# Dilation kernel: seven row sides on TensorE and ScalarE, half merges into pair tiles, 24 GpSimd pairs

## The chip, the cores and the metric

The kernel runs on one core of a Trainium2 chip. Its time is the device time of one execution in microseconds; the time before is 10253.23 us, the median of 3 runs (10250.52 to 10257.87).

## What is computed

The input x has shape 8 x 32 x 256 x 256, fp32. The reference does two residual steps:

```
x = x + dilation(gn(x))      # grey dilation, 11 x 11 taps
x = x + conv(gn(x))          # 1x1 projection, 3x3 depthwise, batch norm, gelu, offsets, bilinear resampling

dilation: acc = max over 121 taps (di, dj) of  pad(u)[y + di, x + dj] - k[channel, di, dj]
```

gn is a group norm with 16 groups of two channels. Since it is a scale and a shift per image and group, the kernel dilates the raw x with k times the standard deviation and scales the result at the end.

## The kernel before

The 256 planes (8 images x 32 channels) lie on 128 partitions in two groups. The kernel has four stages: statistics and tables (to about 200 us), the dilation (to about 8685 us), the convolution and the resampling. The change is in the dilation.

**Tiling.** A window u holds 16 rows of output with 5 rows and columns of border on each side; two windows alternate. A window is done in two chunks of 8 rows x 256 columns, so a chunk's tile is 128 x 2048 fp32. There are 64 chunks. For each window GpSimd also makes dx = u shifted by one column minus u (`difference`, L192).

**Pairs.** Two neighbouring taps of a row can be merged as max(u0 - k0, u1 - k1) = u0 + relu(u1 - u0 + k0 - k1) - k0. ScalarE makes the relu from dx (`pair_relu`, L621), the addition of u is done either by a DMA that accumulates in SBUF (16 "y" pairs in four t tiles, `add_u`, L501) or by GpSimd (`pair`, L530) in four m tiles. For the pairs in CLAMPED GpSimd makes the first part itself by a min and a max (`clamp`, L518), and then adds (L526). VectorE merges the tile into acc_a in PSUM with one instruction, (tile - k) max acc_a (`merge`, L718; the first merge of a chunk, L715, has no max). Single taps ("s") are merged straight from u.

**Chains.** One side of a row, 5 or 6 taps, can also be done as a chain in PSUM: ScalarE does the relu (`chain_step`, L639), TensorE adds the next dx or u by an identity matmul (`add_step`, L589), and so on. A chain is done in two halves of 4 rows (chain0, chain1). Before, there are six: one left with 4 steps, five right with 5 steps, 29 steps for each half. At a chain's end VectorE merges the half into a second accumulator acc_b in SBUF (`merge_chain`, L692, 128 x 1024). acc_b is started by ScalarE from one single tap (`start_b`, L606), and at the end of the chunk a join takes the maximum of both accumulators (L725), after which x1 is made (L731). SyncE stores x1 and loads the next windows.

**What sets the order.** Each engine works in order. Four strings list what each does in one chunk: ACT_ORDER (x relu for a DMA pair, r relu for a GpSimd pair, 0 and 1 chain steps of the halves, b start of acc_b, u the square sum of x1), PE_ORDER, DVE_ORDER (m, y, s merges, 0 and 1 chain merges) and POOL_ORDER (i issue of an accumulating DMA, c clamp, t addition, d pieces of dx for the next window). Semaphores bind them: an addition waits for its relu or clamp, a merge for its tile, a relu or clamp for the merge that frees its buffer (`a_free`), a chain's first step for VectorE's merge of the chain before on that half.

Of the kernel before, what the change touches and what calls it, by code (L numbers as in the profile page):

```python
# [70 lines left out]
def dilation_taps():  # L75

    pairs, singles = [], []
    for di in range(KS):
        side = dict(CHAINS).get(di)
        if side == "left":  # L80
            pairs += [(di, 5, 6), (di, 7, 8), (di, 9, 10)]
        elif side == "right":
            pairs += [(di, 1, 0), (di, 3, 2)]
            singles += [(di, 4)]
# [3 lines left out]
    while len(pairs) > NPOOL + len(CLAMPED) + NDMA:  # L88
# [269 lines left out]
def dilation(nc, x_pl, x1_pl, ident, kt, nkt, gap_r, gap_l, rstd, shift1, sums1,  # L358
# [3 lines left out]
    D_TURNS = POOL_ORDER.count("d")  # L362
    pool_pairs, dma_pairs, (init_b, *singles) = dilation_taps()
    NPAIR = NPOOL + len(CLAMPED)

# [8 lines left out]
    def col(di, dj):  # L374
        return di * KS + dj


    chain_steps = []
    for ch, (di, side) in enumerate(CHAINS):
        bases = range(1, 5) if side == "left" else range(9, 4, -1)  # L380
        chain_steps += [(ch, step, base) for step, base in enumerate(bases)]
# [8 lines left out]
    with ExitStack() as ctx:  # L390
# [8 lines left out]
        t = [sb(f"t{s}", [P, CR, UC]) for s in range(TP)]  # L399
        acc_b = sb("acc_b", [P, CR, W])  # L400
        x1 = sb("x1", [P, CR, W])
# [16 lines left out]
        chain_taken = [sem(f"chain_taken{h}") for h in range(2)]  # L418
        b_started = sem("b_started")
        a_done = sem("a_done")  # L420
        merged = sem("merged")
        joined = sem("joined")
        act_turns, sp_turns, dve_turns, pool_turns = (sem(f"{e}_turns") for e in ("act", "sp", "dve", "pool"))

        def m_tile(j):

            di, base, outer = pool_pairs[j]
            first = (di * UC + base + 2) % 4
            return m_tiles[j % MP][:, :, first:first + W]

        def at(c, per_chunk, count):
# [20 lines left out]
        with nc.Block() as block:  # L452
# [114 lines left out]
            def _(pe):  # L567
# [8 lines left out]
                def add_step(c, s, k, h, i):  # L576
                    ch, step, base = chain_steps[i]
                    di, side = CHAINS[ch]
# [12 lines left out]
                    added.then_inc(chain_added[h], 1)  # L591
# [9 lines left out]
            def _(act):  # L601
                def start_b(c, s, k):
                    di, dj = init_b

                    act.wait_ge(merged, at(c, 1, 0))
                    nc.scalar.activation(acc_b[:], u[s][:, k * CR + di:k * CR + di + CR, dj:dj + W], ACT.Identity,  # L606
                                         bias=nkt[:, g, col(di, dj):col(di, dj) + 1]).then_inc(b_started, 1)

                def square_before(c, shift_column):
# [15 lines left out]
                def chain_step(c, s, k, h, i):  # L625
                    ch, step, base = chain_steps[i]
                    di, side = CHAINS[ch]
                    right = side == "right"
# [15 lines left out]
                for g in range(GROUPS):  # L644
                    with nc.Fori(0, WIN // 2, engines=ACT_ONLY, hint_back_edge=True) as i:
                        for s in range(2):
                            n = i * 2 + (g * WIN + s)
                            for k in range(CPW):
# [4 lines left out]
                                for kind, j in numbered(ACT_ORDER):  # L653
                                    if kind in "01":
                                        chain_step(c, s, k, int(kind), j)
                                    elif kind == "r":

                                        act.wait_ge(a_done, a_free(c, "m", relu_pairs[j], NPAIR, MP))
                                        pair_relu(s, k, pool_pairs[relu_pairs[j]], m_tile(relu_pairs[j])) \
                                            .then_inc(m_begun, 1)  # L660
                                    elif kind == "x":

                                        act.wait_ge(a_done, a_free(c, "y", j, NDMA, TP))
                                        pair_relu(s, k, dma_pairs[j], t[j % TP][:, :, 0:W]).then_inc(t_ready, 1)
                                    elif kind == "b":
                                        start_b(c, s, k)
                                    else:
                                        square_before(c, n + k)
# [3 lines left out]
            def _(dve):  # L672
                for s in range(TP):
                    nc.vector.memset(t[s][:, :, W:UC], 0.0)
                nc.vector.tensor_scalar(neg_ident[:], ident, -1.0, None, ALU.mult)
                nc.vector.memset(x1[:], 0.0).then_inc(pads_set, 1)
                dve.sem_inc(a_done, NA)
                dve.sem_inc(merged, 1)
                dve.sem_inc(joined, 1)
                for h in range(2):  # L680
                    dve.sem_inc(chain_taken[h], NCHAIN)

                def merge_chain(c, h, ch):
                    di, side = CHAINS[ch]
                    base = col(di, chain_steps[last_step[ch]][2])
                    part = acc_b[:, h * HR:(h + 1) * HR, :]

                    dve.wait_ge(chain_added[h], c * NSTEP + (last_step[ch] + 1))
                    dve.wait_ge(chain_taken[h], at(c, NCHAIN, ch))
                    if ch == 0:  # L690
                        dve.wait_ge(b_started, c + 1)
                    nc.vector.scalar_tensor_tensor(out=part, in0=chain[h][:], scalar=kt[:, g, base:base + 1], in1=part,  # L692
                                                   op0=ALU.subtract, op1=ALU.max).then_inc(chain_taken[h], 1)

                def merge(c, s, k, kind, j):
                    if kind == "m":
                        dve.wait_ge(m_ready, c * NPAIR + (j + 1))
                        di, base, outer = pool_pairs[j]
                        if j in CLAMPED:
                            base = outer  # L700
                        src = m_tile(j)
                    elif kind == "y":
                        dve.wait_ge(t_added[j % TP], c * (len(range(j % TP, NDMA, TP)) * 16) + (j // TP + 1) * 16)
                        passed(dve, dve_turns)
                        di, base, outer = dma_pairs[j]
                        src = t[j % TP][:, :, 0:W]
                    else:
                        di, base = singles[j]
                        src = u[s][:, k * CR + di:k * CR + di + CR, base:base + W]
                    k_base = kt[:, g, col(di, base):col(di, base) + 1]  # L710
                    done = a_after[kind, j]
                    if done == 1:
                        dve.wait_ge(joined, at(c, 1, 0))
                        passed(dve, dve_turns)
                        nc.vector.tensor_scalar(acc_a[:], src, k_base, None, ALU.subtract).then_inc(a_done, 1)  # L715
# [4 lines left out]

                def join(c, s, k):
                    dve.wait_ge(a_done, at(c, NA, NA))
                    for h in range(2):
                        dve.wait_ge(chain_taken[h], at(c, NCHAIN, NCHAIN))
                    nc.vector.tensor_tensor(acc_a[:], acc_a[:], acc_b[:], ALU.max).then_inc(merged, 1)  # L725

                    dve.wait_ge(x1_squared, c + 1)
                    dve.wait_ge(merged, at(c, 1, 1))
                    passed(dve, dve_turns)
                    top = k * CR + R  # L730
# [4 lines left out]
                for g in range(GROUPS):  # L735
                    with nc.Fori(0, WIN // 2, engines=DVE_ONLY, hint_back_edge=True) as i:
                        for s in range(2):
                            for k in range(CPW):
# [9 lines left out]
                                join(c, s, k)  # L748

# [744 lines left out]
```

## Time and profile before

| | |
|---|---|
| profiled execution | 10254.56 us, span 10252.8 us |
| median of 3 runs | 10253.23 us |
| VectorE busy | 9963.9 us, 97% of the span |
| ScalarE busy | 9179.9 us, 90% |
| GpSimd busy | 8875.6 us, 87% |
| TensorE busy | 8565.8 us, 84% |

DVE is VectorE, ACT ScalarE, POOL GpSimd, PE TensorE, SP SyncE. A share is busy time over the whole span. The busy time of an engine is the time covered by records of its instructions; where two records overlap it counts once. A wait is put down to the instruction that ended last before it.

### The profile page before, as it was taken

The numbers are of one execution on the slowest core, as the hardware profiler recorded it, in microseconds if no ns is written. First come the engines' busy times: TensorE is split into PE (matmuls) and PEld (weight loads), VectorE is DVE, ScalarE is ACT, GpSimd is POOL, SyncE is SP. The second block draws the span as 40 slices with busy tenths as digits, with TensorE's granted clock in tenths as the row PEclk, the third lists the DMA queues.
The fourth block names the chain that finished last, engine by engine and source line by source line (L and its number), as shares of the span: only waits on it lengthen the run. The fifth ranks groups of instructions, "written<-read, shape, count | busy, mean of one in ns | idle before, by whom it ended". The sixth has DMA issues, their size and how long they took to land. (4 is left out here: it accounts for less than half of the span.)

```text
span 10252.8 us, 72623 instructions
## 1 busy us (share of the span) xinstructions
PE 8565.8 (84%) x18068; PEld 3322.9 (32%) x18068; DVE 9963.9 (97%) x5623; ACT 9179.9 (90%) x6861; POOL 8875.6 (87%) x3274
## 2 busy tenths in 40 slices
PE   2888888888888888888888888888888887998899
PEld 0333333333333333333333333333333333443333
DVE  8999999999999999999999999999999999999999
ACT  2999999999999999999999999999999997888776
POOL 2889888898988999898988888898889887777998
PEclk9999999999999999999999999999999999999999
DMA  8788878888888888888888888888888876444776
GB/s 322 149 157 151 155 155 159 158 160 158 159 157 159 159 158 159 153 159 156 160 155 156 159 158 160 159 158 157 160 159 158 158 141 137 178 182 187 268 282 258
DMA packets 442070, 1751.43 MB, mean 171 GB/s; under 512 B 23888, under 2 KB 130384, under 8 KB 392784
## 3 DMA queue, kind: packets, MB, share of 16 engines
q0 software_dynamic: 278528, 1110.51, 60.9%
q1 hardware_dynamic: 163152, 636.41, 16.6%
q8 instruction: 160, 2.62, 0.1%
q14 instruction: 230, 1.88, 0.0%
HBM read 391.58 MB, written 201.33 MB: 58 GB/s over the span
## 5 line engine op out<-in xcount | busy, mean ns | idle before, releaser
L589 PE MATMUL chain<-dx,mats 128*128 128x512 f32 x10240 | 4979.5, 632 | 940.6 <-ACT chain L639 940.3
L530 POOL TENSOR_TENSOR m<-m,u 128x2048 f32<-128x2048 f32 x1024 | 4338.1, 4350 | 187.1 <-ACT m L621 185.9
L589 PEld LDWEIGHTS chain<-dx,mats 128*128 128x128 f32 x10240 | 1917.0, 197 | 4002.9 <-ACT chain L639 2095.8
L718 DVE SCALAR_TENSOR_TENSOR acc_a<-m,kt,acc_a 128x2048 f32<-128x2048 f32 x1344 | 3162.5, 2353 | 38.2 <-issue 2.4
L639 ACT ACTIVATE chain<-chain,gap_r 128x1024 f32<-128x1024 f32 x2560 | 2694.2, 1086 | 232.2 <-PE chain L589 230.5
L718 DVE SCALAR_TENSOR_TENSOR acc_a<-t,kt,acc_a 128x2048 f32<-128x2048 f32 x1024 | 2411.9, 2355 | 34.2
L501 POOL DMA_DIRECT2D t<-u x1024 | 1486.4, 1563 | 652.8 <-ACT t L621 635.1
L526 POOL TENSOR_TENSOR m<-u,m 128x2048 f32<-128x2048 f32 x384 | 1707.1, 4445 | 0.0
L621 ACT ACTIVATE t<-dx,gap_l 128x2048 f32<-128x2048 f32 x768 | 1540.5, 2006 | 0.4 <-issue 0.4
L589 PE MATMUL chain<-u,mats 128*128 128x512 f32 x3072 | 1456.0, 605 | 71.8 <-ACT chain L639 71.8
L718 DVE SCALAR_TENSOR_TENSOR acc_a<-u,kt,acc_a 128x2048 f32<-128x2048 f32 x576 | 1357.0, 2356 | 20.5
L621 ACT ACTIVATE m<-dx,gap_l 128x2048 f32<-128x2048 f32 x640 | 1286.3, 2010 | 14.9 <-DVE acc_a L718 13.6
L692 DVE SCALAR_TENSOR_TENSOR acc_b<-chain,kt,acc_b 128x1024 f32<-128x1024 f32 x768 | 966.0, 1279 | 70.8 <-PE chain L589 70.0
L518 POOL TENSOR_SCALAR m<-dx,gap_l 128x2048 f32<-128x2048 f32 x384 | 940.8, 2450 | 68.6 <-DVE acc_a L718 68.4
L589 PE MATMUL chain<-dx,neg_ident 128*128 128x512 f32 x1536 | 735.6, 614 | 315.5 <-ACT chain L639 315.5
L639 ACT ACTIVATE chain<-dx,gap_r 128x1024 f32<-128x1024 f32 x640 | 712.5, 1121 | 238.9 <-DVE acc_b L692 224.2
L589 PEld LDWEIGHTS chain<-u,mats 128*128 128x128 f32 x3072 | 547.2, 188 | 949.9 <-issue 558.9
L621 ACT ACTIVATE m<-dx,gap_r 128x2048 f32<-128x2048 f32 x384 | 767.3, 1998 | 0.0
L1126 DVE SCALAR_TENSOR_TENSOR hp<-o,par,hp 128x1024 f32<-128x1024 f32 x512 | 621.8, 1279 | 8.9 <-PE hp L915 8.8
L621 ACT ACTIVATE t<-dx,gap_r 128x2048 f32<-128x2048 f32 x256 | 516.1, 2016 | 15.1 <-PE chain L572 15.1
L589 PEld LDWEIGHTS chain<-dx,neg_ident 128*128 128x128 f32 x1536 | 271.2, 190 | 779.9 <-ACT chain L639 529.9
L915 PE MATMUL hp<-o,diag 128*128 128x512 f32 x1024 | 464.5, 596 | 24.1 <-DVE h L1126 23.9
(149 smaller groups left out, 6876.4 us busy)
## 6 DMA issues: line engine op xcount, KB each, us to landing
t<-u POOLq DMA_DIRECT2D x1024, 1059.0 KB, 8.7
u<-x_dram SPq DMA_DIRECT2D x32, 2688.0 KB, 30.6
xt<-x_dram SPq DMA_DIRECT2D x32, 2048.0 KB, 14.2
x_scratch<-x SPq DMA_DIRECT2D x64, 1024.0 KB, 10.7
h_scratch<-h SPq DMA_DIRECT2D x32, 2048.0 KB, 7.2
both<-h_scratch SPq DMA_DIRECT2D x64, 1024.0 KB, 9.3
out_dram<-res SPq DMA_DIRECT2D x64, 1024.0 KB, 4.9
both<-x_scratch SPq DMA_DIRECT2D x28, 2304.0 KB, 12.6
```

The source lines that it names most:

```text
L501: nc.gpsimd.dma_start(t[j % TP][:].rearrange("p r w -> p (r w)")[:, 0:RUN], u[s][:].rearrange("p r w -> p (r w)")[:, first:first + RUN], a ...
L518: nc.gpsimd.tensor_scalar(m_tile(j), dx[s][:, top:top + CR, lo:lo + W], high, low, ALU.min, ALU.max).then_inc(m_clamped, 1)
L526: nc.gpsimd.tensor_tensor(m_tile(j), rows, m_tile(j), ALU.add if outer > base else ALU.subtract).then_inc(m_ready, 1)
L530: nc.gpsimd.tensor_tensor(m_tile(j), m_tile(j), rows, ALU.add).then_inc(m_ready, 1)
L589: added = nc.tensor.matmul(chain[h][:, r:r + 2, :], weight, src[:, top:top + 2, dj:dj + W], start=False, stop=True, skip_group_check=True)
L621: return nc.scalar.activation(dst, dx[s][:, k * CR + di:k * CR + di + CR, lo:lo + W], ACT.Relu, bias=gap[:, g, col(di, base):col(di, base) ...
L639: nc.scalar.activation(chain[h][:], src, ACT.Relu, bias=gap[:, g, col(di, base):col(di, base) + 1], scale=scale).then_inc(chain_relu[h], 1)
L692: nc.vector.scalar_tensor_tensor(out=part, in0=chain[h][:], scalar=kt[:, g, base:base + 1], in1=part, op0=ALU.subtract, op1=ALU.max).then_ ...
L718: nc.vector.scalar_tensor_tensor(out=acc_a[:], in0=src, scalar=k_base, in1=acc_a[:], op0=ALU.subtract, op1=ALU.max).then_inc(a_done, 1)
L915: last = nc.tensor.matmul(hp[part % 3][:, r:r + 2, :], diag[:, t, :], o[n % 3][:, top:top + 2, tx:tx + W], start=(t == 0), stop=(t == TAPS ...
L1126: nc.vector.scalar_tensor_tensor(out=out, in0=o[n % 3][:, q * QR + ty:(q + 1) * QR + ty, tx:tx + W], scalar=par[:, COL_DW + t:COL_DW + t + 1],
```

## The change

- CHAINS has seven row sides: one left and five right with 4 steps, one right with 5 steps; again 29 steps for each half. A right side with 4 steps leaves taps 5 and 4 as one more pair, where a side with 5 steps leaves tap 4 single.
- GpSimd's pairs are 24 where they were 22, nine of them by clamp where there were six, so ScalarE's relus for them are 15 where they were 16. The DMA pairs stay 16. Single taps fall from ten (one of them the start of acc_b) to five.
- acc_b, its start on ScalarE and the join are gone. A chain's half is merged into a pair tile (m or y, the second such tile after it in DVE_ORDER): tile half = (chain - (k_chain - k_tile)) max tile half. The tile's own merge into acc_a waits for the halves that go into it. The differences of k (k_gap, 28: one for each group, half and chain) are computed once at the start of the dilation.
- There are five m tiles where there were four. The SBUF that is set aside for descriptors of DMAs issued by GpSimd is 8192 bytes a partition; it was not given before, which means 16384.
- The order strings of ScalarE, TensorE, VectorE and GpSimd are new.

```diff
-CHAINS = ((0, "left"), (1, "right"), (2, "right"), (3, "right"), (4, "right"), (5, "right"))
-NPOOL, NDMA = 16, 16
-CLAMPED = (1, 5, 9, 12, 16, 20)
-MP, TP = 4, 4
-ACT_ORDER = "x0x01r01xr10b1r01r01x01x01r01xr0u10r10x10x10x1r01r01r01x01x01x01r01r01x01r01rx010r10x10r10x1"
-PE_ORDER = "0011010101010101010101010101010101010101010101010101010101"
-DVE_ORDER = "m01mmymysss0m1myysymmy01mmsmyyms01msymsymm01ymymyysm0m1mymy"
-POOL_ORDER = "iitcitttcitittittcitdititcittiicttditittictitt"
+CHAINS = ((0, "left", 4), (1, "right", 4), (2, "right", 4), (3, "right", 4), (4, "right", 4), (5, "right", 4), (6, "right", 5))
+NPOOL, NDMA = 24, 16
+CLAMPED = (0, 2, 7, 8, 14, 17, 18, 20, 22)
+MP, TP = 5, 4
+ACT_ORDER = "xx01r01x0101r0r10r10x10r1x0x10r10r10r1xx01r01r01x01rx01r01x0101x01x01x01r01xr01x01u01r0101"
+PE_ORDER = "0101010101010101010101010101010101010101010101010101010101"
+DVE_ORDER = "m01mysmmy0m1ymsmmy01mymymmm01yymmsy01mymmyy01ymmssmmy01ymmy"
+POOL_ORDER = "iicttictttctictitittiiittctittittidicctititctdiitctt"
...
+def chain_targets():
+    targets = {}
+    order = list(numbered(DVE_ORDER))
+    for place, (kind, ch) in enumerate(order):
+        if kind in "01":
+            tiles = [x for x in order[place + 1:] if x[0] in "my"]
+            targets[int(kind), ch] = tiles[:2][-1]
+    return targets
...
+                for g in range(GROUPS):
+                    for (h, ch), tile in targets.items():
+                        last = col(CHAINS[ch][0], chain_steps[last_step[ch]][2])
+                        other = tile_col(*tile)
+                        nc.vector.tensor_tensor(k_gap[:, g, 2 * ch + h:2 * ch + h + 1], kt[:, g, last:last + 1],
+                                                kt[:, g, other:other + 1], ALU.subtract).then_inc(k_gap_ready, 1)
...
+                def merge_chain(c, h, ch):
+                    tile = targets[h, ch]
+                    part = tile_of(*tile)[:, h * HR:(h + 1) * HR, :]
+                    dve.wait_ge(chain_added[h], c * NSTEP + (last_step[ch] + 1))
+                    tile_ready(c, *tile)
+                    if ch > 0 and targets[h, ch - 1] == tile:
+                        dve.wait_ge(chain_taken[h], at(c, NCHAIN, ch))
+                    nc.vector.scalar_tensor_tensor(out=part, in0=chain[h][:],
+                                                   scalar=k_gap[:, g, 2 * ch + h:2 * ch + h + 1], in1=part,
+                                                   op0=ALU.subtract, op1=ALU.max).then_inc(chain_taken[h], 1)
...
-                    nc.vector.tensor_tensor(acc_a[:], acc_a[:], acc_b[:], ALU.max).then_inc(merged, 1)
...
-    nc = bacc.Bacc("TRN2", target_bir_lowering=False, num_devices=1)
+    nc = bacc.Bacc("TRN2", target_bir_lowering=False, num_devices=1,
+                   dynamic_dma_scratch_size=8192)
```

## Rows read from the trace of the kernel before

**Rows 1.** Page, part 1: busy time of each engine, share, instructions.

```profile
PE 8565.8 (84%) x18068; PEld 3322.9 (32%) x18068; DVE 9963.9 (97%) x5623; ACT 9179.9 (90%) x6861; POOL 8875.6 (87%) x3274
```

**Rows 2.** One line of the code, L731: durations (ns), first and last start (us).

```profile
L731 DVE SCALAR_TENSOR_TENSOR x<-acc_a,small,u x64: 2349/2351/2352, 350.8 to 8682.7; 128x2048 f32<-128x2048 f32 x64
```

**Rows 3.** Windows: length, busy PE, PEld, DVE, ACT, POOL, clock, DMA share.

```profile
2000.00:4000.00 2000.00, 1685.76 (x3514) 645.95 (x3513) 1955.36 (x940) 1880.76 (x1408) 1791.72 (x698) 0.97 0.82 159
```

**Rows 4.** Waits, 400 to 7500 us: total us, times, longest.

```profile
POOL t L501 <- ACT t L621: 517.5, 268, 4.0
...
ACT chain L639 <- DVE acc_b L692: 194.5, 191, 2.1
POOL m L530 <- ACT m L621: 148.5, 151, 2.1
POOL m L518 <- DVE acc_a L718: 57.2, 54, 1.2
DVE acc_b L692 <- PE chain L589: 52.9, 131, 0.8
DVE x L731 <- DVE acc_a L725: 12.9, 54, 0.2
...
DVE acc_a L725 <- DVE acc_a L718: 10.7, 54, 0.2
```

**Rows 5.** Timeline of VectorE, 4003 to 4017 us: start, length, instruction.

```profile
4004.14 2.36 DVE L718 SCALAR_TENSOR_TENSOR acc_a<-u,kt,acc_a 128x2048 f32<-128x2048 f32 x1
4006.53 2.36 DVE L718 SCALAR_TENSOR_TENSOR acc_a<-t,kt,acc_a 128x2048 f32<-128x2048 f32 x1
...
4013.58 2.47 DVE L692 SCALAR_TENSOR_TENSOR acc_b<-chain,kt,acc_b 128x1024 f32<-128x1024 f32 x2
4015.96 2.35 DVE L718 SCALAR_TENSOR_TENSOR acc_a<-t,kt,acc_a 128x2048 f32<-128x2048 f32 x1
```

**Rows 6.** Groups by line, 400 to 7500 us: busy, mean ns, idle before.

```profile
L725 DVE TENSOR_TENSOR acc_a<-acc_a,acc_b 128x2048 f32<-128x2048 f32 x54 | 124.1, 2299 | 10.7 <-DVE acc_a L718 10.7
...
L606 ACT ACTIVATE acc_b<-u,nkt 128x2048 f32<-128x2048 f32 x54 | 108.4, 2007 | 0.0
```

**Rows 7.** Timeline of GpSimd, 3109 to 3145 us, a stretch without a wait.

```profile
3110.86 1.21 POOL L501 DMA_DIRECT2D t<-u  x1 [0.80 <-ACT t L621]
3111.65 4.27 POOL L526 TENSOR_TENSOR m<-u,m 128x2048 f32<-128x2048 f32 x1
3115.44 4.25 POOL L530 TENSOR_TENSOR m<-m,u 128x2048 f32<-128x2048 f32 x1
3119.19 2.89 POOL L501 DMA_DIRECT2D t<-u  x2
3120.79 5.13 POOL L530 TENSOR_TENSOR m<-m,u 128x2048 f32<-128x2048 f32 x1
3124.62 3.25 POOL L518 TENSOR_SCALAR m<-dx,gap_l 128x2048 f32<-128x2048 f32 x1
3126.53 2.51 POOL L501 DMA_DIRECT2D t<-u  x1
3127.96 4.93 POOL L526 TENSOR_TENSOR m<-u,m 128x2048 f32<-128x2048 f32 x1
3131.72 8.71 POOL L530 TENSOR_TENSOR m<-m,u 128x2048 f32<-128x2048 f32 x2
3139.34 3.04 POOL L518 TENSOR_SCALAR m<-dx,gap_l 128x2048 f32<-128x2048 f32 x1
```

**Rows 8.** Timeline of GpSimd in the resampling; the second needs the first.

```profile
9499.38 3.81 POOL L1354 TENSOR_TENSOR dv<-y 128x2048 f32<-128x2048 f32 x1
9503.27 3.60 POOL L1358 TENSOR_TENSOR dd<-dv 128x2048 f32<-128x2048 f32 x1
```

**Rows 9.** Groups by line, whole span: small subtractions and products of VectorE.

```profile
L311 DVE TENSOR_TENSOR small<-small 128x2 f32<-128x2 f32 x1 | 1.9, 1875 | 0.0
...
L327 DVE TENSOR_TENSOR gap_r<-kt 128x120 f32<-128x120 f32 x2 | 0.6, 284 | 0.1
```

**Rows 10.** Page, parts 3 and 6: queue of GpSimd's DMAs; KB each, us to landing.

```profile
q0 software_dynamic: 278528, 1110.51, 60.9%
...
t<-u POOLq DMA_DIRECT2D x1024, 1059.0 KB, 8.7
```

More of the change, by code:

```diff
@@ L77, in dilation_taps @@
     pairs, singles = [], []
+    sides = {di: (side, links) for di, side, links in CHAINS}
     for di in range(KS):
-        side = dict(CHAINS).get(di)
+        side, links = sides.get(di, (None, 0))
         if side == "left":
@@ L83, in dilation_taps @@
             pairs += [(di, 1, 0), (di, 3, 2)]
-            singles += [(di, 4)]
+            if links == 4:
+                pairs += [(di, 5, 4)]
+            else:
+                singles += [(di, 4)]
         else:
@@ L87, in dilation_taps @@
             singles += [(di, 10)]
-    while len(pairs) > NPOOL + len(CLAMPED) + NDMA:
+    while len(pairs) > NPOOL + NDMA:
         di, base, outer = pairs.pop()
@@ L362, in dilation @@
     D_TURNS = POOL_ORDER.count("d")
-    pool_pairs, dma_pairs, (init_b, *singles) = dilation_taps()
-    NPAIR = NPOOL + len(CLAMPED)
+    pool_pairs, dma_pairs, singles = dilation_taps()
+    targets = chain_targets()
+    NPAIR = NPOOL
     relu_pairs = [j for j in range(NPAIR) if j not in CLAMPED]
@@ L378, in dilation @@
     chain_steps = []
-    for ch, (di, side) in enumerate(CHAINS):
-        bases = range(1, 5) if side == "left" else range(9, 4, -1)
+    for ch, (di, side, links) in enumerate(CHAINS):
+        bases = range(1, 1 + links) if side == "left" else range(9, 9 - links, -1)
         chain_steps += [(ch, step, base) for step, base in enumerate(bases)]
@@ L399, in dilation @@
         t = [sb(f"t{s}", [P, CR, UC]) for s in range(TP)]
-        acc_b = sb("acc_b", [P, CR, W])
+        k_gap = sb("k_gap", [P, GROUPS, 2 * NCHAIN])
         x1 = sb("x1", [P, CR, W])
@@ L418, in dilation @@
         chain_taken = [sem(f"chain_taken{h}") for h in range(2)]
-        b_started = sem("b_started")
+        k_gap_ready = sem("k_gap_ready")
         a_done = sem("a_done")
-        merged = sem("merged")
         joined = sem("joined")
@@ L429, in m_tile, with tile_of, tile_col @@
             return m_tiles[j % MP][:, :, first:first + W]
+        def tile_of(kind, j):
+            return m_tile(j) if kind == "m" else t[j % TP][:, :, 0:W]
+        def tile_col(kind, j):
+            di, base, outer = pool_pairs[j] if kind == "m" else dma_pairs[j]
+            return col(di, outer if kind == "m" and j in CLAMPED else base)
         def at(c, per_chunk, count):
@@ L577, in add_step @@
                     ch, step, base = chain_steps[i]
-                    di, side = CHAINS[ch]
+                    di, side, _ = CHAINS[ch]
                     pe.wait_ge(chain_relu[h], c * NSTEP + (i + 1))
@@ L601, in _ @@
             def _(act):
[L602 to L607, printed above, removed]
                 def square_before(c, shift_column):
@@ L626, in chain_step @@
                     ch, step, base = chain_steps[i]
-                    di, side = CHAINS[ch]
+                    di, side, _ = CHAINS[ch]
                     right = side == "right"
@@ L681, in _, with tile_ready @@
                     dve.sem_inc(chain_taken[h], NCHAIN)
+                def tile_ready(c, kind, j):
+                    if kind == "m":
+                        dve.wait_ge(m_ready, c * NPAIR + (j + 1))
+                    else:
+                        dve.wait_ge(t_added[j % TP], c * (len(range(j % TP, NDMA, TP)) * 16) + (j // TP + 1) * 16)
                 def merge_chain(c, h, ch):
-                    di, side = CHAINS[ch]
-                    base = col(di, chain_steps[last_step[ch]][2])
@@ L686, in merge_chain @@
-                    part = acc_b[:, h * HR:(h + 1) * HR, :]
+                    tile = targets[h, ch]
+                    part = tile_of(*tile)[:, h * HR:(h + 1) * HR, :]
                     dve.wait_ge(chain_added[h], c * NSTEP + (last_step[ch] + 1))
[L689 to L692, printed above, removed]
+                    tile_ready(c, *tile)
@@ L710, in merge @@
-                    k_base = kt[:, g, col(di, base):col(di, base) + 1]
+                    if kind == "s":
+                        di, base = singles[j]
+                        src, at_col = u[s][:, k * CR + di:k * CR + di + CR, base:base + W], col(di, base)
+                    else:
+                        tile_ready(c, kind, j)
+                        src, at_col = tile_of(kind, j), tile_col(kind, j)
+                        for h in range(2):
+                            taken = [ch for (half, ch), tile in targets.items() if half == h and tile == (kind, j)]
+                            if taken:
+                                dve.wait_ge(chain_taken[h], at(c, NCHAIN, max(taken) + 1))
@@ L711, in merge @@
+                    k_base = kt[:, g, at_col:at_col + 1]
                     done = a_after[kind, j]
@@ L719, in merge, with finish @@
                                                        op0=ALU.subtract, op1=ALU.max).then_inc(a_done, 1)
-                def join(c, s, k):
+                def finish(c, s, k):
+                    dve.wait_ge(x1_squared, c + 1)
                     dve.wait_ge(a_done, at(c, NA, NA))
-                    for h in range(2):
-                        dve.wait_ge(chain_taken[h], at(c, NCHAIN, NCHAIN))
-                    nc.vector.tensor_tensor(acc_a[:], acc_a[:], acc_b[:], ALU.max).then_inc(merged, 1)
-                    dve.wait_ge(x1_squared, c + 1)
-                    dve.wait_ge(merged, at(c, 1, 1))
-                    passed(dve, dve_turns)
                     top = k * CR + R
@@ L747, in _ @@
                                         merge(c, s, k, kind, j)
-                                join(c, s, k)
+                                finish(c, s, k)
 def load_resampled(sp, x1_pl, h_pl, hw, xw, hw_loaded, xw_loaded, n, what):
```

19 lines of the change are left out of this document (2 added, 17 removed).

## Prediction

> **What bounds the kernel now.** I read the engine totals first [rows 1]: VectorE is busy for 97% of the span, ScalarE 90%, GpSimd 87%, TensorE 84%. The change touches only the dilation, so its period comes next: the x1 update at the end of a chunk runs 64 times, from 350.8 to 8682.7 us [rows 2], which is 8331.9 / 63 = 132.25 us a chunk and 64 x 132.25 = 8464 us of the 10252.8. In a stretch of 2000 us inside it [rows 3] (15.12 chunks) VectorE is busy for 1955.4 us, 129.3 a chunk, ScalarE 124.4, GpSimd 118.5, TensorE 111.5. The table of waits of 7100 us (53.7 chunks) [rows 4] says the same from the other side. VectorE waits in the three rows shown for 52.9 + 12.9 + 10.7 us, with some smaller ones 1.5 us a chunk; GpSimd waits for 517.5 + 148.5 + 57.2 us, 13.5 a chunk, and with small rows 13.7. So VectorE is the bound with 130.8 us of work in 132.25, and GpSimd has 13.7 us to spare. What the change is worth depends on how much of these 13.7 us it uses up.
>
> **VectorE.** Full merges fall by two (m 22 to 24, singles s 9 to 5, y 16 as before). Two of them start 2.39 us apart [rows 5], so -4.78. The join with the second accumulator goes: 2.30 us [rows 6] and the 10.7 / 54 = 0.2 us that it waited for the merge before it, -2.50. Two chain merges are added (12 to 14); two of them take 2.38 us from start to next start [rows 5], +2.38. They read PSUM and write a pair tile where they wrote acc_b; shape and memories are those of the old ones, so I take the same price. Sum -4.9: VectorE needs 130.8 - 4.9 = 125.9 us a chunk. Were it still the bound, with its old 1.5 us of waits, the period would be 127.4.
>
> **ScalarE and TensorE.** The start of acc_b goes (2.007 us [rows 6]) and one relu of a pair, which has the same shape: -4.0, so 124.4 falls to 120.4. The chain steps stay 58 (29 for each half: before 4 + 5 x 5, now 6 x 4 + 5), so TensorE keeps its 111.5. A seventh chain means two more first steps that wait for VectorE's merge; ScalarE now waits so for 194.5 us in 53.7 chunks [rows 4], 3.6 a chunk for twelve such steps, so +0.6 us. That fits into its 11 us of slack and costs nothing.
>
> **GpSimd.** This is where the price lies. Its 22 additions become 24 and its 6 clamps 9; the 16 DMA issues and the two pieces of dx a chunk stay. The records of following instructions overlap on this engine, so I time it over a stretch without a wait [rows 7]: from 3110.86 to the end of the last record, 3139.34 + 3.04 = 3142.38, there are 31.52 us with 6 additions, 4 issues and 2 clamps. An addition advances the next start by 3.77 (3115.44 to 3119.19 shows 3.75, the row before it 3.79), a clamp by 1.91 (3124.62 to 3126.53). That leaves (31.52 - 22.62 - 3.82) / 4 = 1.27 for an issue. Check on the whole chunk: 22 x 3.77 + 6 x 1.91 + 16 x 1.27 + two pieces of about 1.95 = 118.6, where the windows say 118.5. So the rates hold. The change adds 2 x 3.77 + 3 x 1.91 = 13.3. One thing is new in its order: four clamps (pairs 0, 2, 20, 22) stand directly before their own addition, which must wait for the clamp's end. In the resampling an instruction that needs the one before starts 0.08 us after its end [rows 8] where others start 0.04 or more before it; 4 x 0.12 = 0.5. Sum: 118.5 + 13.3 + 0.5 = 132.3 us. GpSimd becomes the bound, and its work alone fills the old period of 132.25. What VectorE saves can't be cashed.
>
> The Trainium skill (GPSIMD Engine Reference, section 3.1) gives 4497 ns for an addition of 2048 fp32 on GpSimd, against 2293 on VectorE. The rows here have 3.77 us, and the row decides. By the page's figure the two new additions would cost 0.73 us more each, some 93 us over 64 chunks. Its section 4.1 advises against moving elementwise work to this engine, which is what this change does.
>
> What it still waits: the old bound engine waited 1.5 us a chunk. For the new one I followed the loop that looks tightest through the order strings. The merge of chain 6 goes into pair 22, whose addition ends when all but the last one of GpSimd's chunk is done, at 131.9 - 3.77 = 128.1 of its count (131.9: the chunk's sum by the rates above). VectorE then has two chain merges, four merges and the x1 update to do, 2 x 1.19 + 4 x 2.39 + 2.7 = 14.6, and in the next chunk up to the merge of pair 2 another 5 x 2.39 + 2 x 1.19 = 14.3: 157.0, which is 25.1 on GpSimd's next count. The clamp of pair 7 needs the tile that this merge frees, and stands after 3 issues, 2 clamps and 5 additions, at 26.5: free, but by 1.4 us only. Later clamps and relus reuse tiles whose merges stand further back. So I take 0.7 us a chunk, between 0 and the 1.5 of before: period 133.0, +0.75 x 64 = +48 us.
>
> **The rest.** 28 tiny subtractions for k_gap run once before VectorE opens the semaphores. The nearest row is a subtraction of 120 columns, 0.284 us; a product of 2 columns took 1.875 [rows 9]. Ends: nothing and 28 x 1.875 = 52 us; no instruction there waits for the one before, and one column is less than 120, so I take 5 (0.18 each). The halved scratch for DMA descriptors I cost at nothing, in the third rival. Convolution and resampling keep their code. Against the profiled execution's 10254.6 us: + 48 + 5 = 10307.6; the median of the runs lies 1.3 lower, so 10306.
>
> **Rivals.**
> 1. *GpSimd is not so full; VectorE stays the bound.* By starts alone the stretch of [rows 7] takes 3139.34 + 1.91 - 3110.86 = 30.39 us, an issue 0.99, and the chunk 114.1; the new one needs 127.4 with the 13.3, just what VectorE does. If the late ends of records are no work that holds up the next ones, the period is 127.4: 10254.6 - 4.85 x 64 + 5 = 9949, which is faster. Against it: the late ends repeat after every issue, and only with them does the sum meet the windows' 118.5. Chance 0.20.
> 2. *The three orders lock into each other.* A chain merge now needs the chain's last matmul and a tile two places ahead, and the tile's own merge needs both halves. With GpSimd full, VectorE comes late to chain merges, ScalarE's first steps wait for these, and relus come late to GpSimd, which has no slack to catch up. It decides once the 1.4 us of margin named above are gone. Price: as much idle time as a quarter of GpSimd's present waits, 3.5 us a chunk: 10254.6 + (0.05 + 3.5) x 64 + 5 = 10487. For it: 9.6 us of GpSimd's waits now are for relus of DMA pairs [rows 4]; against: ScalarE gains 4 us. Chance 0.14.
> 3. *The smaller scratch makes issues wait for landed transfers.* A transfer lands 8.7 us after issue; 16 issues a chunk each waiting for the one before would add over 100 us a chunk, thousands in all. 278528 packets in 1024 transfers [rows 10] are 272 each, 17 per DMA engine, and at most four transfers are open, since there are four t tiles. No row shows how many fit. The Trainium skill (DMA: Bandwidth & Descriptors, SWDGE vs HWDGE vs iDMA) puts the rings into that part of SBUF, with 16-byte descriptors; 8192 bytes would be 512 of them, room for 30 transfers (an estimate from the page). Chance 0.02.
>
> **Numbers.** Forecast (GpSimd bound, period 132.0 to 134.5) 0.64, its own range 10240 to 10405 us. Within it: slower by over 0.2% (20 us, about what a measurement tells from no change, 0.3 us a chunk) 0.43, same 0.17, faster 0.04. With the rivals: faster 0.24, same 0.17, slower 0.59. The range leaves out rival 1's lower part the top of rival 2 and rival 3, and takes in the higher price of k_gap: 10070 to 10430.
>
> **What would show it.** In the windows of the changed kernel GpSimd is busy for 131 to 133 us a chunk and over 98% of the time, its waits for relus of DMA pairs (517.5 us) nearly gone; VectorE drops to some 124.5 us busy a chunk, with several us of waits for m tiles or chains, where it had none. Times of one merge and one addition stay. Wrong would be: GpSimd busy under 129 a chunk (rival 1), or a GpSimd that is busy under 97% with a period above 135 (rival 2).

## The result and the profile after

The changed kernel takes 10293.12 us (median of 6 runs, 10287.45 to 10295.78), the kernel before 10251.61 (median of 6 runs as well). The ratio is 1.0039, with a 95% interval of 1.0026 to 1.0052: slower by about 40 us. The forecast was 10306 us, range 10070 to 10430. The profiled execution has a span of 10291.0 us. The string POOL_ORDER of the kernel that ran is iicttictttctictitittiitttctitittidicctititctdiitctt, with 16 issues; the one printed with the change has one i too many and one t in another place.

In the lines below L520 issues a DMA, L537 is a clamp, L545 and L549 are GpSimd's additions (L545 after a clamp), L633 is ScalarE's relu of a pair and L651 that of a chain, L608 is TensorE's step, L713 merges a chain half into a tile, L736 merges a tile or a single tap into acc_a and L204 makes dx. In the kernel with small clamps the numbers above L545 are one lower.

The engine totals of the changed kernel, against [rows 1]:

```profile
PE 8545.1 (83%) x18068; PEld 3365.9 (33%) x18068; DVE 9678.9 (94%) x5587; ACT 8957.3 (87%) x6733; POOL 9735.8 (95%) x3594
```

GpSimd has passed VectorE. The x1 update, against [rows 2], gives the period: (8717.0 - 345.5) / 63 = 132.88 us a chunk, where it was 132.25.

```profile
L743 DVE SCALAR_TENSOR_TENSOR x<-acc_a,small,u x64: 2351/2351/2353, 345.5 to 8717.0; 128x2048 f32<-128x2048 f32 x64
```

The span grew by 38.2 us: 39.6 in these 63 periods, -5.3 before the first update, +3.9 behind the last one.

Windows of the changed kernel inside the dilation (busy PE, PEld, DVE, ACT, POOL, then clock and DMA share), against [rows 3]:

```profile
2000.00:4000.00 2000.00, 1672.76 (x3491) 653.15 (x3490) 1877.47 (x920) 1819.09 (x1370) 1985.71 (x769) 0.96 0.82 158
4000.00:6000.00 2000.00, 1668.57 (x3481) 651.41 (x3480) 1871.06 (x916) 1813.31 (x1366) 1982.73 (x769) 0.96 0.81 154
6000.00:8000.00 2000.00, 1675.40 (x3496) 654.30 (x3495) 1878.39 (x919) 1818.83 (x1371) 1986.10 (x769) 0.96 0.82 158
```

GpSimd is busy for 99.2% of these 6000 us. In a period of 132.88 that is 131.9 us, and 1.0 idle. VectorE has 124.6 us busy, ScalarE 120.7. The waits of 400 to 7500 us, against [rows 4], show the change of sides: what GpSimd waited for is nearly gone, and VectorE now waits for GpSimd's additions, for chains and for DMA tiles. ScalarE waits less for VectorE's chain merges (66.0 us, where it was 194.5) and more for TensorE (514.8 us, where it was 203.0).

```profile
ACT chain L651 <- PE chain L608: 514.8, 532, 3.0
DVE t L713 <- PE chain L608: 106.1, 118, 4.0
DVE acc_a L736 <- POOL m L545: 96.4, 68, 2.3
...
ACT chain L651 <- DVE t L713: 58.8, 79, 3.3
DVE acc_a L736 <- POOL m L549: 55.4, 104, 2.2
DVE t L713 <- DMA t<-u: 53.9, 44, 3.2
DVE m L713 <- POOL m L545: 50.8, 50, 1.0
...
POOL m L537 <- DVE acc_a L736: 31.8, 24, 2.9
ACT chain L651 <- DVE m L713: 7.2, 25, 0.3
...
POOL t L520 <- ACT t L633: 3.9, 3, 2.3
```

GpSimd's own timeline, against [rows 7], shows how full it is. Start, length, instruction:

```profile
3092.82 5.64 POOL L545 TENSOR_TENSOR m<-u,m 128x2048 f32<-128x2048 f32 x1
3096.56 3.06 POOL L520 DMA_DIRECT2D t<-u  x1
3097.34 6.13 POOL L549 TENSOR_TENSOR m<-m,u 128x2048 f32<-128x2048 f32 x1
3101.14 4.27 POOL L537 TENSOR_SCALAR m<-dx,gap_l 128x2048 f32<-128x2048 f32 x1
3105.50 3.83 POOL L545 TENSOR_TENSOR m<-u,m 128x2048 f32<-128x2048 f32 x1
3109.28 1.96 POOL L204 TENSOR_TENSOR dx<-u 128x1060 f32<-128x1060 f32 x1
```

The addition at 3097.34 has a record of 6.13 us, though the next instruction starts 3.80 us later. The record of the clamp after it ends at 3105.41, 4.27 us after its start, and the addition that needs this clamp starts at 3105.50, 0.09 after that end. So the late end counts: the overhang of 2.3 us that has piled up behind several DMA issues (it grows by about 0.45 at each) is paid there. The Trainium skill (GPSIMD Engine Reference, sections 2.1 and 4) says that a core of this engine goes on to the next instruction without waiting for the others, and that a pair of cores generates the DMA descriptors; by that rule these two would lag after each issue. The trace agrees as far as overhang and pay-back go, but doesn't show the cores apart.

An overhang also hides waits, because the tables count as idle only the time that no record covers. Earlier in the same chunk:

```profile
3078.19 4.38 POOL L520 DMA_DIRECT2D t<-u  x1
3078.97 5.59 POOL L204 TENSOR_TENSOR dx<-u 128x1060 f32<-128x1060 f32 x1
3083.56 2.15 POOL L520 DMA_DIRECT2D t<-u  x1
```

The issue at 3083.56 starts 4.59 us after the piece of dx, though such a piece advances GpSimd by 1.9 (3109.28 to 3111.17). It starts 0.58 us after the end of its relu on ScalarE (3080.99 + 1.99 = 3082.98). So stands the twelfth issue in nearly all chunks. It comes 2.1 us late in the mean, while late records still run, and the overhang shrinks from 2.8 to 1.2 us meanwhile. By the late records nothing is lost; but GpSimd's room against ScalarE is smaller than the 3.9 us in the table suggest.

### The profile page after: what moved, and what is told of

Read it like the earlier page. It is cut to its first block and busy times, and to the rows that moved or that the text cites. A ratio compares the mean times of both kernels' runs of the same rounds, so it can differ in the third digit from the quotient of the medians.

```text
span 10291.0 us, 73426 instructions
## 1 busy us (share of the span) xinstructions
PE 8545.1 (83%) x18068; PEld 3365.9 (33%) x18068; DVE 9678.9 (94%) x5587; ACT 8957.3 (87%) x6733; POOL 9735.8 (95%) x3594
## 3 DMA queue, kind: packets, MB, share of 16 engines
q0 software_dynamic: 278528, 1110.51, 61.1%
q1 hardware_dynamic: 163152, 636.41, 16.7%
## 5 line engine op out<-in xcount | busy, mean ns | idle before, releaser
L608 PE MATMUL chain<-dx,mats 128*128 128x512 f32 x9728 | 4723.5, 630 | 1075.4 <-ACT chain L651 1075.4
L549 POOL TENSOR_TENSOR m<-m,u 128x2048 f32<-128x2048 f32 x960 | 4379.7, 5021 | 0.0
L736 DVE SCALAR_TENSOR_TENSOR acc_a<-m,kt,acc_a 128x2048 f32<-128x2048 f32 x1472 | 3465.9, 2355 | 215.6 <-POOL m L545 111.8
L608 PEld LDWEIGHTS chain<-dx,mats 128*128 128x128 f32 x9728 | 1813.8, 196 | 3984.9 <-ACT chain L651 2154.5
L651 ACT ACTIVATE chain<-chain,gap_r 128x1024 f32<-128x1024 f32 x2432 | 2566.3, 1084 | 405.9 <-PE chain L608 405.0
L545 POOL TENSOR_TENSOR m<-u,m 128x2048 f32<-128x2048 f32 x576 | 2645.8, 4685 | 21.3
L736 DVE SCALAR_TENSOR_TENSOR acc_a<-t,kt,acc_a 128x2048 f32<-128x2048 f32 x1024 | 2410.6, 2354 | 27.3
L520 POOL DMA_DIRECT2D t<-u x1024 | 2132.7, 2222 | 23.2 <-ACT t L633 22.8
L537 POOL TENSOR_SCALAR m<-dx,gap_l 128x2048 f32<-128x2048 f32 x576 | 1667.3, 3069 | 38.4 <-DVE acc_a L736 38.4
L608 PE MATMUL chain<-u,mats 128*128 128x512 f32 x3584 | 1659.4, 599 | 50.6 <-ACT chain L651 50.6
L633 ACT ACTIVATE t<-dx,gap_l 128x2048 f32<-128x2048 f32 x832 | 1660.5, 2005 | 45.8 <-DVE acc_a L736 41.7
L633 ACT ACTIVATE m<-dx,gap_l 128x2048 f32<-128x2048 f32 x576 | 1156.9, 2008 | 0.0
L608 PE MATMUL chain<-dx,neg_ident 128*128 128x512 f32 x1536 | 787.5, 665 | 262.1 <-ACT chain L651 187.1
L608 PEld LDWEIGHTS chain<-u,mats 128*128 128x128 f32 x3584 | 655.0, 188 | 1003.4 <-issue 629.8
L651 ACT ACTIVATE chain<-dx,gap_r 128x1024 f32<-128x1024 f32 x768 | 847.4, 1121 | 82.0 <-DVE t L713 69.7
L713 DVE SCALAR_TENSOR_TENSOR t<-chain,k_gap,t 128x1024 f32<-128x1024 f32 x576 | 725.6, 1281 | 196.3 <-PE chain L608 130.3
L633 ACT ACTIVATE m<-dx,gap_r 128x2048 f32<-128x2048 f32 x384 | 769.3, 2003 | 0.0
L736 DVE SCALAR_TENSOR_TENSOR acc_a<-u,kt,acc_a 128x2048 f32<-128x2048 f32 x320 | 753.9, 2356 | 11.4
L204 POOL TENSOR_TENSOR dx<-u 128x1060 f32<-128x1060 f32 (+1 forms) x134 | 461.2, 3468 | 172.3 <-DMA u<-x_dram 172.3
L651 ACT ACTIVATE chain<-chain,gap_l 128x1024 f32<-128x1024 f32 x384 | 409.3, 1082 | 210.1 <-PE chain L608 210.1
L608 PEld LDWEIGHTS chain<-dx,neg_ident 128*128 128x128 f32 x1536 | 310.7, 210 | 738.9 <-issue 425.7
## 6 DMA issues: line engine op xcount, KB each, us to landing
t<-u POOLq DMA_DIRECT2D x1024, 1059.0 KB, 10.4
```

What stands on the lines that cost most here:

```text
L204: nc.gpsimd.tensor_tensor(dx[buf][:, lo:hi, 0:UC - 1], u[buf][:, lo:hi, 1:UC], u[buf][:, lo:hi, 0:UC - 1], ALU.subtract).then_inc(dx_ready, 1)
L520: nc.gpsimd.dma_start(t[j % TP][:].rearrange("p r w -> p (r w)")[:, 0:RUN], u[s][:].rearrange("p r w -> p (r w)")[:, first:first + RUN], a ...
L537: nc.gpsimd.tensor_scalar(m_tile(j), dx[s][:, top:top + CR, lo:lo + W], high, low, ALU.min, ALU.max).then_inc(m_clamped, 1)
L545: nc.gpsimd.tensor_tensor(m_tile(j), rows, m_tile(j), ALU.add if outer > base else ALU.subtract).then_inc(m_ready, 1)
L549: nc.gpsimd.tensor_tensor(m_tile(j), m_tile(j), rows, ALU.add).then_inc(m_ready, 1)
L633: return nc.scalar.activation(dst, dx[s][:, k * CR + di:k * CR + di + CR, lo:lo + W], ACT.Relu, bias=gap[:, g, col(di, base):col(di, base) ...
```

## Experiments

Periods below are from the first and the last x1 update over 63, work is the busy share of the windows times the period. Ratios are against the kernel before.

### GpSimd relieved: small clamps

```diff
-nc.gpsimd.tensor_scalar(m_tile(j), dx[s][:, top:top + CR, lo:lo + W], high, low,
+nc.gpsimd.tensor_scalar(m_tile(j)[:, 0:1, :], dx[s][:, top:top + 1, lo:lo + W], high, low,
...
-nc.gpsimd.tensor_tensor(m_tile(j), rows, m_tile(j), ALU.add if outer > base else ALU.subtract)
+nc.gpsimd.tensor_tensor(m_tile(j), rows, rows, ALU.add)
```

> The changed kernel with each of the nine clamps on one of its eight rows, and the additions of these pairs made as u + u (the same shape, both inputs in SBUF); the nine pairs' values are left out of the result. This takes about 9 x 1.7 = 15 us of work a chunk from GpSimd and nothing from another engine. Theory (GpSimd's work is the bound, 132.2 of 132.88 us a chunk): the period falls until VectorE bounds again, at its 125.9 us of work plus 1 to 2 us of waits, 127 to 128: some 5.4 x 64 = 345 us less than the changed kernel's 10293, so 9950 (9920 to 9990). Rival (the engines lock into each other by the chain merges into tiles, GpSimd only looks full): the waits stay, the period falls by less than 2 us, and the time stays above 10160.

Measured: 10048.05 us, ratio 0.9799 (0.9783 to 0.9816), period 129.06. Its windows and its longest waits of VectorE and GpSimd:

```profile
2000.00:4000.00 2000.00, 1699.73 (x3593) 660.39 (x3592) 1933.80 (x947) 1866.96 (x1411) 1804.61 (x789) 0.98 0.84 162
...
POOL t L520 <- ACT t L632: 348.6, 266, 3.8
POOL m L537 <- DVE acc_a L735: 200.8, 55, 3.7
DVE t L712 <- PE chain L607: 140.1, 210, 1.7
```

With 15 us less to do GpSimd waits again and the period falls by 3.8 us: GpSimd was the bound of the changed kernel, and a saving was there behind it. It is smaller than expected: the time lies above the range of 9920 to 9990, and the period is 129.06 and not 127.4. VectorE, with 124.8 us busy, now waits 2.8 us a chunk, nearly all of it for chains (140.1 us and a row of 12.9, in 55 chunks); the kernel before had 1.5 us of waits, 1.0 of them for chains. In both kernels another 1.5 us a chunk are neither busy nor in the table of waits.

### VectorE relieved: no single taps

```diff
-DVE_ORDER = "m01mysmmy0m1ymsmmy01mymymmm01yymmsy01mymmyy01ymmssmmy01ymmy"
+DVE_ORDER = "m01mymmy0m1ymmmy01mymymmm01yymmy01mymmyy01ymmmmy01ymmy"
```

> The changed kernel without its five single taps on VectorE (five of the 121 taps are left out of the result). VectorE has 5 x 2.39 = 12 us a chunk less to do. Theory (GpSimd is the bound): nothing, 10293 within 15 us, and VectorE's waits grow by 12 us a chunk. Rival (VectorE or the loop through its merges still sets the period): a fall of 2 to 12 us a chunk, 130 to 770 us.

Measured: 10272.03 us, ratio 1.0019 (1.0009 to 1.0028), period 132.60; the changed kernel had 132.88. Twelve microseconds of VectorE's work are worth 0.3. VectorE's share falls from 94% to 85%, GpSimd's is 99.4%. The 21 us are a bit more than the 15 I allowed: they come from GpSimd's own 1.0 us of idle time, for its clamps' waits for VectorE's merges fell from 31.8 us to 0.2.

### The scratch alone

```diff
 nc = bacc.Bacc("TRN2", target_bir_lowering=False, num_devices=1,
+               dynamic_dma_scratch_size=8192)
```

> The kernel before with the descriptor scratch at 8192 bytes and nothing else changed. Theory: no change, 10252 within 10 us, the issues of the accumulating DMAs keep their shortest records (1.14 us) and their 8.7 us to landing. Rival (fewer descriptors fit, so that issues wait): longer issue records and over 100 us more.

Measured: 10248.64 us, ratio 0.9995 (0.9985 to 1.0005); issues keep 1138 ns at least, and 8.7 us to landing. So the third rival is ruled out in the kernel before. In the changed kernel it wasn't tried alone, but the shortest issue takes 1131 ns with 8192 bytes and, in the next run, 1146 ns with 16384. Transfers do land later in the changed kernel, 10.4 us after their issue (9.7 in the next run); why was not tried. VectorE's waits for these tiles are 53.9 us, 1.0 a chunk.

### Four m tiles

```diff
-MP, TP = 5, 4
+MP, TP = 4, 4
...
-               dynamic_dma_scratch_size=8192)
```

> The changed kernel with four m tiles where it has five, and the descriptor scratch at its default of 16384 bytes. The clamp of pair 7 now waits for the merge of pair 3 (2.4 to 7 us later in VectorE's order than pair 2) with a margin of 1.4 us before. Theory: GpSimd, which has no slack, waits about 1 us a chunk for VectorE (clamps on merges), so +60 us, 10350 (10310 to 10420). Rival (buffers don't matter, every free tile is early): 10293 within 10 us.

Measured: 10546.79 us, ratio 1.0286 (1.0268 to 1.0303), period 136.83. The fifth tile is worth 4.0 us a chunk here, four times what I expected. GpSimd has the same 131.9 us of work, and waits again (51.9 chunks):

```profile
POOL m L537 <- DVE acc_a L736: 139.6, 52, 5.4
DVE acc_a L736 <- POOL m L545: 122.6, 103, 3.2
POOL t L520 <- ACT t L633: 82.8, 89, 4.7
```

One clamp a chunk waits for the merge that frees its tile (52 times, 2.7 us), as the loop of the prediction says. Then the lateness goes round: relus of DMA pairs come late too. Since the scratch alone cost nothing in the kernel before, the tile is taken as the cause.

### GpSimd's slack before: clamps done twice

```diff
+pool.wait_ge(m_clamped, c * (2 * len(CLAMPED)) + (2 * i + 1))
+passed(pool, pool_turns)
+nc.gpsimd.tensor_scalar(m_tile(j), dx[s][:, top:top + CR, lo:lo + W], high, low,
+                        ALU.min, ALU.max).then_inc(m_clamped, 1)
```

> The kernel before with each of its six clamps done twice, the second after the first, the same result. GpSimd gets 6 x (1.91 + 0.12) = 12.2 us more work a chunk, 130.7 of a period of 132.25 in which it had 13.7 us of waits. Theory of the prediction (a slack is free as long as the sum fits the period): within 1 us a chunk, 10252 to 10316. Rival (the slack sits at certain places, and a buffer's round trip is made longer by the extra clamp): a period of 134 to 140, 10370 to 10750.

Measured: 10370.31 us, ratio 1.0117 (1.01 to 1.0134), period 133.98. The period grows by 1.7 us for 12 us of added work. The theory's 1 us is missed, and the rival's lower end is just met. So most of the slack of 13.7 us is real, but its last part wasn't usable: 3.7 us of waits stay.

```profile
POOL t L501 <- ACT t L625: 98.3, 61, 2.6
POOL m L522 <- POOL m L518: 67.6, 318, 0.2
```

The second row is the new clamp waiting for the one before it, 0.21 us each and 1.3 a chunk; the other 2.5 are mostly for ScalarE's relus. (In this kernel L501 is the issue, L518 the first clamp and L522 the second.)

### One clamp less

```diff
-CLAMPED = (0, 2, 7, 8, 14, 17, 18, 20, 22)
+CLAMPED = (0, 2, 8, 14, 17, 18, 20, 22)
-ACT_ORDER = "xx01r01x0101r0r10r10x10r1x0x10r10r10r1xx01r01r01x01rx01r01x0101x01x01x01r01xr01x01u01r0101"
+ACT_ORDER = "xx01r01x0101r0r10r10x10r1xr0x10r10r10r1xx01r01r01x01rx01r01x0101x01x01x01r01xr01x01u01r0101"
-POOL_ORDER = "iicttictttctictitittiitttctitittidicctititctdiitctt"
+POOL_ORDER = "iictticttttictitittiitttctitittidicctititctdiitctt"
```

> The changed kernel with one clamp less: pair 7 gets its relu from ScalarE (one r more behind that of pair 6, one c less on GpSimd), all else in place. Theory (GpSimd's work is the bound): it loses 1.91 + 0 us a chunk, ScalarE gains 1.9 and stays at 123: period 131.0, 10293 - 1.9 x 64 = 10172. If the new relu comes late to the addition of pair 7 or delays the relu of DMA pairs behind it, part of it is lost: up to 10270. Rival (no bound of its own, a loop through ScalarE): 10293 or more.

Measured: 10367.73 us, ratio 1.0116 (1.0099 to 1.0133), period 134.07: slower than the changed kernel by 75 us, and a miss. GpSimd's work did fall, to 130.1 us. But it waits 3.6 us a chunk for relus of DMA pairs:

```profile
POOL t L520 <- ACT t L633: 189.1, 103, 6.4
```

In its timeline these are two issues that follow each other:

```profile
3070.02 5.17 POOL L549 TENSOR_TENSOR m<-m,u 128x2048 f32<-128x2048 f32 x1
3077.22 1.21 POOL L520 DMA_DIRECT2D t<-u  x1 [2.04 <-ACT t L633]
3079.11 1.20 POOL L520 DMA_DIRECT2D t<-u  x1 [0.68 <-ACT t L633]
```

The added relu stands on ScalarE ahead of the chain steps and of the relus of the next DMA pairs. Counted from the first issue of the chunk, the relu of the seventh issue started at 49.0 us in the changed kernel and starts at 51.7 here, while GpSimd arrives 1.9 us earlier than it did. A bound engine was relieved by an engine that still had idle time, and the time rose, because the receiver's work has a place and not only a length. Another place for the relu was not tried.

### Three descriptors a row

```diff
-accum_op=ALU.add, max_dma_last_dim=RUN // 2 * 4)
+accum_op=ALU.add, max_dma_last_dim=RUN // 3 * 4)
```

> The changed kernel with each accumulating DMA cut into three pieces a row where it has two (a third more than half again as many packets, the same bytes). It tests whether what an issue costs GpSimd, 1.27 us with the late end of its record, grows with the descriptors. Theory: the issue is work that holds up what follows; if it goes with the descriptors it becomes 1.9, +0.6 x 16 = 10 us a chunk, 10930; if half of it is fixed, 10610. Rival (the late end of the record holds nothing up): 10293 within 30 us.

Measured: 10382.22 us, ratio 1.0129 (1.0112 to 1.0146), period 134.25. Packets rise from 278528 to 409600 (400 a transfer where it was 272). GpSimd is busy for 133.4 us, +1.5 us over 16 issues, 0.09 each. So longer issues do hold the engine up, and nearly nothing of it is hidden (+1.4 us in the period). But the price hardly goes with the descriptors: 1.27 becomes 1.36, not 1.9. The two figures of the theory were far too high, and the rival's 30 us are missed too (89).

### Merging into tiles alone

Six sides, 22 pairs, the old orders without b, with one more s; the rest as in the changed kernel.

```diff
+CHAINS = ((0, "left", 4), (1, "right", 5), (2, "right", 5), (3, "right", 5), (4, "right", 5), (5, "right", 5))
+NPOOL, NDMA = 22, 16
+CLAMPED = (1, 5, 9, 12, 16, 20)
+DVE_ORDER = "m01mmymyssss0m1myysymmy01mmsmyyms01msymsymm01ymymyysm0m1mymy"
```

> One part of the change alone: six row sides, 22 GpSimd pairs and six clamps as before, in the old orders, but chain halves are merged into pair tiles, the second accumulator, its start on ScalarE and the join are gone, the tap that started it is a single on VectorE, with five m tiles and a scratch of 8192 bytes. VectorE loses 2.5 us a chunk (join) and gets 2.39 (the tap); ScalarE loses 2.0; GpSimd keeps 118.5. Theory (VectorE is the bound here, and a merge into a tile costs what one into the accumulator did): 132.1 us a chunk, 10245 (10220 to 10270). Rival (merging into tiles couples the engines by itself): VectorE waits 1 to 3 us a chunk for tiles or chains, 10310 to 10440.

Measured: 10956.85 us, ratio 1.0689 (1.0671 to 1.0707), period 143.3. The rival is right, and at four times its price. VectorE stands before chain merges whose m tile isn't ready (the last two rows):

```profile
POOL t L520 <- ACT t L633: 808.9, 281, 7.2
...
ACT chain L651 <- DVE m L713: 440.6, 197, 4.7
...
DVE m L713 <- POOL m L549: 325.3, 49, 7.1
DVE m L713 <- POOL m L545: 245.2, 51, 5.5
```

The last two rows are 570.5 us in 49.5 chunks, 11.5 a chunk, as much as the whole loss of 11.0. An accumulator is always there; a pair tile two places ahead makes VectorE wait for work that it needed only later. The first two rows close a loop: ScalarE waits for the chain merges, its relus come late to GpSimd, and GpSimd's additions late to VectorE. That is the second rival of the prediction. In the changed kernel's order nearly all of this is gone: nine of the fourteen chain merges go into DMA tiles, and for the five into m tiles VectorE waits 50.8 us in 53 chunks. It isn't the kind of tile that decides, but its place in the order: in the fastest kernel below eleven of fourteen go into m tiles, and it waits 50.0 us for their additions.

### The same work in another order

```diff
-POOL_ORDER = "iicttictttctictitittiitttctitittidicctititctdiitctt"
+POOL_ORDER = "icittdcititictctittitttiittcttictictititctictitdtit"
```

The strings of ScalarE and VectorE are new too.

> The changed kernel with the same work on every engine and other order strings for ScalarE, VectorE and GpSimd. Theory (GpSimd's 131.9 us of work are the bound and already 99.3% full): at most the 0.9 us a chunk that are left can be won, 10235 to 10300. Rival (the order, not the work, sets 132.9): a fall of 2 us a chunk or more, below 10170.

Measured: 10730.45 us, ratio 1.0465 (1.0448 to 1.0483), period 139.9, a miss. The first piece of dx stands at place 6, before the load of the next window has landed:

```profile
POOL dx L204 <- DMA u<-x_dram: 401.1, 24, 17.3
```

16.7 us in every window, 8.4 a chunk; the period is 7.0 longer than that of the changed kernel. It says nothing on how good the rest of the order is.

### Seven clamps, twice

The first of the two kernels, with clamps (0, 2, 8, 14, 17, 20, 22) and new strings for all four engines:

> The changed kernel with seven clamps where it has nine (pairs 7 and 18 get a relu from ScalarE) and all four order strings laid anew for it. Work a chunk: GpSimd 131.9 - 3.8 = 128.1, ScalarE 120.4 + 3.8 = 124.2, VectorE 125.9. Theory: the period falls to 128.5 to 130.5, bounded by GpSimd or by VectorE's waits for chains: 10020 to 10150, faster than both kernels. Rival (two engines near the bound wait for each other, so nothing is won over the changed kernel's 132.9): 10250 or more.

Measured: 10268.92 us, ratio 1.0017 (1.0007 to 1.0027), period 132.59. That is 24 us less than the changed kernel, but far above the 10020 to 10150 expected, and the rival's 10250 or more is met. GpSimd's work is 128.0 us as expected, but its last piece of dx stood last in the order, and ScalarE's first relu of a window needs it:

```profile
POOL t L520 <- ACT t L633: 191.0, 95, 4.5
ACT m L633 <- POOL dx L204: 182.1, 26, 8.2
```

The second differs in GpSimd's string alone. The last piece goes from place 49 to 42 and the first from 42 to 40 (the expectation gives other numbers of places; the string is what ran):

```diff
-POOL_ORDER = "cittcitttititctitititttciitittctitittcitiditcittd"
+POOL_ORDER = "cittcitttititctitititttciitittctitittcidtdiitcitt"
```

> The kernel with seven clamps of the run before, with the last piece of dx of the next window moved forward by ten places in GpSimd's order, and the first one back by two. There ScalarE waited for that piece for 182.1 us in 7100 us, 3.4 a chunk, at the first relu of every window. Theory: these waits go, GpSimd has 128.1 us of work, VectorE 125.9: period 129.0 to 130.5, 10060 to 10150, faster than both kernels. Rival (the chains' loop through the three engines sets 132): 10230 or more.

Measured: 10181.66 us, ratio 0.9932 (0.9915 to 0.9948), period 131.19: faster than both kernels, by 70 us against the one before and 111 against the changed one, though short of what I expected. The waits for dx, 3.4 us a chunk, are gone, but the period fell by 1.4 only; others took the rest of their place:

```profile
ACT chain L651 <- DVE m L713: 160.2, 204, 3.8
...
POOL m L537 <- DVE acc_a L736: 92.7, 51, 4.1
POOL t L520 <- ACT t L633: 81.3, 64, 3.7
```

GpSimd is busy for 127.9 of 131.19 us.

### One pair less

```diff
-NPOOL, NDMA = 24, 16
-CLAMPED = (0, 2, 7, 8, 14, 17, 18, 20, 22)
+NPOOL, NDMA = 23, 16
+CLAMPED = (0, 2, 7, 8, 14, 17, 18, 20)
```

with new strings.

> The changed kernel with 23 GpSimd pairs where it has 24 and eight clamps where it has nine: the last pair becomes two single taps on VectorE, with new orders. GpSimd loses 3.77 + 1.91 = 5.7 us a chunk (126.4), VectorE gets 2.39 (128.3), ScalarE keeps its 120.4. Theory: VectorE with some waits bounds at 129.5 to 132, 10090 to 10240, faster than the changed kernel. Rival (any pair moved only trades one wait for another, since the chains' loop sets the period): 10280 or more.

Measured: 10267.15 us, ratio 1.0016 (1.0006 to 1.0026), period 132.3. The time lies between the two ranges. Work is near what was reckoned, 126.2 us on GpSimd and 127.0 on VectorE, yet neither fills the period: on either 5 to 6 us a chunk are idle. Balanced work is 26 us faster than the changed kernel and still 16 slower than the kernel before, in the order that I found.

## Why the prediction was right

**The bound.** The step that carried it was the sum on GpSimd: 118.5 + 13.3 + 0.5 = 132.3 us; measured 131.9 busy, which is the sum without the 0.5 for waits on own clamps, since such a wait is idle time. The 1.0 idle is what the prediction put at 0.5 + 0.7: the four own clamps cost 0.08 us each, 0.3, and 0.6 stand before the clamp of pair 7, the place that the prediction named. The period of 133.0 came out as 132.88.

**The late ends (rival 1).** By starts alone GpSimd would have needed 127.4. The clamp whose user starts 0.09 us after its late end, and the run with three descriptors, where 1.5 us more of busy time became 1.4 us of period, show that late ends are paid. What the prediction didn't see is that waits for ScalarE can lie under them (2.1 us before the twelfth issue).

**VectorE.** 4.9 us less were forecast, and 124.5 busy; it has 124.6. That this can't be cashed is shown from both sides: 12 us less work on VectorE moves the period by 0.3, 15 us less on GpSimd by 3.8. What was mis-sized is the worth of the saving, 127.4 against a measured 129.06: the chains' waits, which I had put on ScalarE alone (0.6 us, costing nothing), reach VectorE as soon as it is the bound. On ScalarE the forecast went the wrong way: its waits for VectorE's chain merges fell from 3.6 to 1.2 us a chunk where 0.6 more were expected, and those for TensorE rose from 3.8 to 9.6. Neither cost anything in the changed kernel.

**The margins (rival 2).** It did not decide in the changed kernel; the clamps' waits for merges, 31.8 us in 53 chunks, are 0.6 a chunk. But its mechanism is real and nearer than my 0.14 suggests: one tile less, one relu moved or the old orders with merges into tiles, each brought it up. The price of 3.5 us was near in two of these (4.0 with four tiles, 3.6 of waits with one clamp less) and far too low in the third (11.0).

**Small terms.** The 28 differences took 2.0 us, not 5:

```profile
L691 DVE TENSOR_TENSOR k_gap<-kt x28: 95/157/159, 192.8 to 194.6; 128x1 f32<-128x1 f32 x28
```

The first x1 update came 5.3 us earlier, where 5 us more were forecast; the cause was not tried. The tail grew by 3.9, which wasn't forecast either. So the profiled execution is 14.8 us below the 10307.6: 8.4 from the period (39.6 us where 48 were reckoned), 10.3 from the time before the first update, less the 3.9 of the tail. The start and the tail were not foreseen and cancel in part; that much of the agreement is luck.

**What stays open.** I can say which engine was full, and that one kernel with less work on it and another order wins 111 us. That kernel differs in clamps and in all four orders at once, so the 111 us are not divided between them. How much of the 129.06 of the small clamps a kernel with all its work can reach was not found; three of my four new order sets brought a wait of their own.

## What to carry to other kernels

When work moves to an engine with spare time, add up that engine's work against the period first, with rates taken from a stretch in which it never waits, and by the ends of its records where they overlap. If the sum reaches the old period, the gain elsewhere can't show. And slack isn't fungible: a tile that an instruction borrows, or a place in an in-order queue, can cost several times the length of the work (a piece of dx of 1.9 us at a wrong place cost some 8 us a chunk), so read after each move which wait took the place of the last one.

## What the runs showed of the hardware

- The overhang of GpSimd's records grows with each DMA issue while the engine is full, to 2.3 us in the stretch above, and is paid at the next instruction that waits for this engine's own result. Under it an issue can wait 2.1 us for ScalarE without a trace in the table of waits.
- Half as many packets again (400 for 272 in a transfer) make an issue on GpSimd only 0.09 us dearer.
- Halving the scratch for descriptors changes nothing in the kernel before, with up to four transfers open (0.9985 to 1.0005).
